# Adding a graph bias once, as a constant matrix in VectorE's copy, in place of bias matmuls in the coefficient steps

## What is computed

```python
# stage 1: eight Euler steps, linear in h
h = x @ fc_in_w.T + fc_in_b
alph = sigmoid(alpha_train)[:, None]
w_eff = w * clip(d, 0, 1) @ w.T
for _ in range(8):
    ax = adj @ h                                   # over nodes
    f = alph * 0.5 * (ax - h) + h @ w_eff - h + x0 # x0 = x
    h = h + 0.125 * f
x = layernorm(x + h)
# stage 2: four-head attention, 32 channels a head, edges with adj == 0 masked
q, k, v = split(x @ W)
out = softmax(q @ k.T / sqrt(32) + mask) @ v
x = layernorm(x + out)
```

## Time and profile before

| what | value |
|---|---|
| median of three runs | 682.69 us |
| the profiled execution | 683.51 us |
| its span, first to last instruction | 681.7 us |
| instructions in the span | 11846 |
| TensorE matmuls | 646.5 us busy, 95%, 3441 matmuls |
| VectorE, ScalarE, GpSimd | 456.5, 452.1 and 72.9 us busy |
| distance of the items' first PV, 180 to 625 us | 37.1 us, twelve times (one 37.3) |
| chain that ended last | TensorE 85%, VectorE 8%, issue 3% |
| mean granted TensorE clock | 0.989 of full |

### The profile page before, as it was taken

The page is one execution under the profiler, slowest core; times in us unless marked ns, Lnnn a source line. Parts: engine busy times, 40 slices in busy tenths (PEclk is TensorE's granted clock), DMA queues, the critical chain, the costliest instruction groups (busy, mean ns, idle before and its releaser), DMA issues.

```text
span 681.7 us, 11846 instructions
## 1 busy us (share of the span) xinstructions
PE 646.5 (95%) x3441; PEld 474.3 (70%) x3441; DVE 456.5 (67%) x1308; ACT 452.1 (66%) x1023; POOL 72.9 (11%) x86
## 2 busy tenths in 40 slices
PE   4998799999999999999999999999999999999883
PEld 3776676867777776868686777778686868676541
DVE  3442437568594958677685849485866768496986
ACT  3122146867778686868686776868686868678881
POOL 3110000001010100101010102001010101000001
PEclk9999999999999999999999999999999999999897
DMA  4000021312213130403031221303030312112211
GB/s 112 0 1 16 0 63 47 78 33 67 59 43 83 25 101 12 112 0 100 24 82 41 63 60 36 88 19 104 11 103 10 96 27 73 37 49 62 65 29 48
DMA packets 37695, 35.47 MB, mean 52 GB/s; under 512 B 7840, under 2 KB 24864, under 8 KB 37664
## 3 DMA queue, kind: packets, MB, share of 16 engines
q1 hardware_dynamic: 37664, 35.09, 20.0%
HBM read 5.57 MB, written 4.19 MB: 14 GB/s over the span
## 4 chain that ended last, share of the span: by engine, by line
PE 85%; DVE 8%; issue 3%; ACT 1%; DMA 1%; SPq 0%; POOL 0%; DVEq 0%; POOLq 0%
PE psS L711 9%; PE psO L816 8%; PE psL L697 8%; PE psL L698 8%; PE psL L699 8%; PE psE L801 7%; PE psL L689 5%; PE psL L691 5%; PE psL L690 5%; PE psM L771 4%; PE psE L797 4%; PE psL L762 2%; PE psM L776 2%; PE psS L636 2%; PE psE L636 2%
## 5 line engine op out<-in xcount | busy, mean ns | idle before, releaser
L957 DVE CUSTOM_DVE_ANT_0 Sm<-psS,mask 128x512 f32<-128x512 f32 x256 | 173.1, 687 | 109.2 <-PE psS L711 66.4
L545 ACT ACTIVATE E<-Sm,negmax 128x512 f32<-128x512 f32 x128 | 91.5, 715 | 39.7 <-DVE negmax L957 39.5
L711 PE MATMUL psS<-Ks,Qs 96*128 96x512 f32 x256 | 99.7, 447 | 4.5 <-DVE negmax L957 2.4
L545 ACT ACTIVATE Sm<-Sm,negmax 128x512 f32<-128x512 f32 x128 | 92.4, 727 | 6.6 <-DVE negmax L957 6.6
L588 ACT ACTIVATE ET<-ET 128x512 f32<-128x512 f32 x128 | 77.7, 622 | 0.4 <-DVE ET L992 0.3
L992 DVE TENSOR_TENSOR ET<-psE,maskT 128x512 f32<-128x512 f32 x120 | 77.0, 682 | 1.0 <-PE psE L797 1.0
L478 POOL TENSOR_TENSOR rstd<-var,minus_half 128x4 f32<-128x4 f32 x32 | 32.2, 1007 | 364.9 <-DVE var L940 364.9
L801 PE MATMUL psE<-ident,E 128*128 128x128 f32 x480 | 67.8, 275 | 2.3 <-ACT ET L591 1.5
L591 ACT ACTIVATE ET<-psE 128x512 f32<-128x512 f32 x116 | 68.5, 590 | 0.3 <-PE psE L801 0.3
L711 PEld LDWEIGHTS psS<-Ks,Qs 96*128 96x128 f32 x256 | 45.6, 192 | 28.7 <-issue 14.2
L801 PEld LDWEIGHTS psE<-ident,E 128*128 128x128 f32 x480 | 57.3, 142 | 8.5 <-ACT E L545 1.7
(11 more groups left out here) (158 smaller groups left out, 1100.7 us busy)
## 6 DMA issues: line engine op xcount, KB each, us to landing
Qs<-qh SPq DMA_DIRECT2D x128, 64.0 KB, 2.0
Ks<-kh SPq DMA_DIRECT2D x128, 64.0 KB, 2.0
xin<-in_x_dram SPq DMA_DIRECT2D x16, 256.0 KB, 2.9
...
Qs<-Mh SPq DMA_DIRECT2D x16, 4.0 KB
```

What stands on the lines that cost most here:

```text
L545: nc.scalar.activation(row if h < TH else E[:, h % 2, i, :], row, ACT.Exp, scale=-1.0, bias=negmax[:, h * NT + i:h * NT + i + 1], accum_ou ...
L711: mm(psS[i % 2][:, :], Qs[0:KS, h, i * P:(i + 1) * P], Ks[0:KS, h, :], start=True, stop=True).then_inc(s_mm, 1)
L957: V_.tensor_tensor_reduce(out=Sm[:, i % 2, :], in0=psS[i % 2][:, :], in1=mask[:, i, :], scale=-SCALE, scalar=3e38, op0=ALU.add, op1=ALU.mi ...
```

## The change

The whole bias becomes one 128 by 512 constant `biasT`. It is worked out in the preamble and in pass 0, by matmuls that lie between the units of item 0, and VectorE adds it as it copies `J1` to `YT`. `J0` stays with ScalarE. The matmul of line 684 is gone from all coefficient steps, and so are the factors `rb` and `Wst`. All lists are written anew.

TensorE:

```diff
-            for i in range(PW):
-                for k in range(NT if i else 1):
-                    for part in (PTh, PTl) if i else (spread,):
-                        last = mm(psM[0:3 * QUAD, :], sel[:, i, 0:3 * QUAD], ...
+            def bias_columns(q, pick):
+                rows = slice(q * QUAD, q * QUAD + pick.shape[0])
+                pe.wait_ge(bias_ev, (3, 7)[q])
+                n = pick.shape[1]
+                for t in range(NT):
+                    last = mm(psM[:, t * n:(t + 1) * n], wrow[rows, t * P:(t + 1) * P], pick,
+                              start=True, stop=True)
+                last.then_inc(bias_mm, 1)
+            def bias_rows(q):
+                pe.wait_ge(bias_ev, (2, 6, 9)[q])
+                for k in range(NT):
+                    for part in (PTh, PTl):
+                        last = mm(psM[0:3 * QUAD, :], wcols[q][:, k, 0:3 * QUAD], part[:, PW - 1 if q else 0, k, :],
+                                  start=k == 0 and part is PTh, stop=k == NT - 1 and part is PTl)
+                last.then_inc(bias_mm, 1)
+            def bias_constant():
+                pe.wait_ge(bias_ev, 10)
+                mm(psM[:, :], brow[:, :], wrow[:, :], start=True, stop=True).then_inc(bias_mm, 1)
...
             recurrence(7)
+            bias_rows(0)
             power(2, 1)
...
             power(2, 2)
-            for q in range(BLK):
-                last = mm(psM[0:3 * QUAD, q * D:(q + 1) * D], bcols[:, q, :], ident[:, :], start=True, stop=True)
+            bias_columns(0, fold[0:PW, 0:PW - 1])
+            mm(psM[0:3 * QUAD + 1, P:P + D], bcols[:, :], ident[:, :], start=True, stop=True).then_inc(bias_mm, 1)
...
             def coefficients(it, block):
-                mm(bank, rb[0:3 * QUAD, block, :], Wst[0:3 * QUAD, :], start=True, stop=False)
                 for i in range(PW):
-                    mm(bank, Rh[:, k, :], zh[:, i, :], start=False, stop=False)
+                    mm(bank, Rh[:, k, :], zh[:, i, :], start=i == 0, stop=False)
...
+                        # apply_power calls this between its 6th and 7th matmul, in J1 of item 0
+                        bias_constant if first and n else None
...
+                        if (kind, n) == ("YT", 0):
+                            bias_rows(1)
+                        elif (kind, n) == ("J", 0):
+                            bias_columns(1, fold[QUAD:QUAD + 2 * PW, :])
+                        elif (kind, n) == ("YT", 1):
+                            bias_rows(2)
```

VectorE (pass 0, and the join of every item). In the preamble it also gets two small operations on `wcols`, six small copies and three small operations in place of three copies, and `bias_row`, `bias_split` and a copy to `brow` in place of two subtractions:

```diff
+                        if (kind, n) == ("YT", 1):
+                            bias_row(4, slice(QUAD, QUAD + 2 * PW))
+                            bias_split(2, 5)
+                        elif (kind, n) == ("J", 1):
+                            bias_row(6, slice(2 * QUAD, 2 * QUAD + 2 * PW))
+                            dve.wait_ge(bias_mm, 7)
+                            V_.tensor_copy(biasT[:, :], psM[:, :]).then_inc(bias_ev, 1)
+                            dve.wait_ge(bias_ev, 11)
...
+                    elif kind == "J":
+                        dve.wait_ge(l0_mm, l0_unit(b, (kind, n)) + 1)
+                        bank = L0_BANK[L0_UNITS.index((kind, n))]
+                        V_.tensor_tensor(YT[:, :], psL[bank][:, :], biasT[:, :], ALU.add).then_inc(l0_ev[bank], 1)
```

The lists, new order from the start of a pass (the drain lists are written anew too):

```diff
+PE_EVENTS = [
+    ("S", 2, 0, 2), ("S", 2, 1, 2), ("PV", 0, 0, 3), ("PV", 1, 0, 3), ("PV", 2, 0, 3), ("MT", 0, 0, 2),
+    ("PV", 3, 0, 3), ("S", 2, 2, 2), ("UT", 0, 0, 1), ("Z", 1, 0, 0), ("TR", 0, 0, 2), ("TR", 0, 1, 2),
+    ("XT", 0, 0, 0), ("S", 2, 3, 2), ("X1T", 0, 0, 1), ("CB", 0, 0, 3), ("S", 3, 0, 2), ("TR", 0, 2, 2),
+    ("S", 3, 1, 2), ("Q", 1, 0, 1), ("Z", 2, 0, 0), ("TR", 0, 3, 2), ("S", 3, 2, 2), ("K", 2, 0, 1),
+    ("TR", 1, 0, 2), ("TR", 1, 1, 2), ("C", 2, 0, 0), ("S", 3, 3, 2), ("TR", 1, 2, 2), ("TR", 1, 3, 2),
...
+ACT_EVENTS = [
+    ("TR", 3, 2, 3), ("S", 1, 3, 2), ("TR", 3, 3, 3), ("MT", 0, 0, 2), ("OT", 0, 0, 3), ("S", 2, 0, 2),
+    ("S", 2, 1, 2), ("Z", 1, 0, 0), ("X1T", 0, 0, 1), ("S", 2, 2, 2), ("S", 2, 3, 2), ("XT", 0, 0, 0),
+    ("TR", 0, 0, 2), ("TR", 0, 1, 2), ("Q", 1, 0, 1), ("TR", 0, 2, 2), ("S", 3, 0, 2), ("TR", 0, 3, 2),
...
+DVE_EVENTS = [
+    ("TR", 3, 2, 3), ("MT", 0, 0, 2), ("S", 2, 1, 2), ("LN1A", 0, 0, 1), ("TR", 3, 3, 3), ("S", 2, 2, 2),
+    ("LN1B", 0, 0, 1), ("TR", 0, 0, 2), ("S", 2, 3, 2), ("Z", 1, 0, 0), ("TR", 0, 1, 2), ("S", 3, 0, 2),
+    ("S", 3, 1, 2), ("XT", 0, 0, 0), ("TR", 0, 2, 2), ("QL", 1, 0, 1), ("TR", 0, 3, 2), ("TR", 1, 0, 2),
...
+    ("S", 1, 3, 1), ("J", 1, 0, 0), ("TR", 3, 1, 2), ("S", 2, 0, 1),
...
-    ("XS", 0, 0, 0), ("LN1A", 0, 0, 0), ("KEEP", 0, 0, 0), ("LN2A", 0, 0, 2),
+    ("XS", 0, 0, 0), ("LN1A", 0, 0, 0), ("LN2A", 0, 0, 2), ("KEEP", 0, 0, 0),
...
-    ("STK", 0, 0, 2), ("STK", 1, 0, 2), ("OUT", 0, 0, 4), ("STK", 2, 0, 2), ("STK", 3, 0, 2), ("XIN", 0, 0, 0),
-    ("MT", 0, 0, 2),
+    ("XIN", 0, 0, 0), ("STK", 1, 0, 2), ("STK", 2, 0, 2), ("OUT", 0, 0, 4), ("STK", 3, 0, 2), ("MT", 0, 0, 2),
+    ("STK", 0, 0, 1),
```

More of the change, by code:

```diff
@@ L208, in gnn_kernel @@
         Rl = sb("Rl", [P, RS, D], F32R)
-        rb = sb("rb", [P, BLK, D], F32R)
-        Wst = sb("Wst", [P, N], F32R)
+        biasT = sb("biasT", [P, N])
+        brow = sb("brow", [3 * QUAD + 1, D])
+        fold = sb("fold", [2 * QUAD, PW])
+        rowsum = sb("rowsum", [P, NT])
         W_sb = sb("W_sb", [P, 3 * D])
@@ L243, in gnn_kernel @@
         decay_ident = x1res[:, 1, 3, :]
-        bcols = bass.AP(x1res, NT * D, [list(x1res[:, 0, 0, :].ap[0]), [3 * QUAD, BLK], [1, 3 * QUAD]])
+        bcols = x1res[:, 1, 0, 0:3 * QUAD + 1]
         Sm = sb("Sm", [P, 2, N])
@@ L260, in gnn_kernel @@
         minus_half = sb("minus_half", [P, NT])
+        wrow = att[0:3 * QUAD + 1, :, :].rearrange("p t d -> p (t d)")
+        wcols = [t[:, :].rearrange("p (t c) -> p t c", c=P) for t in (kh, qh, ql)]
         Rst = bass.AP(ET, 0, [list(ET[:, 0, 0, :].ap[0]), [(RS + 1) * SLOT, 2], [SLOT, RS + 1], [1, SLOT]])
@@ L306, in gnn_kernel @@
         bias_mm = sem("bias_mm")
-        bias_hi = sem("bias_hi")
-        bias_lo = sem("bias_lo")
+        bias_ev = sem("bias_ev")
+        w_sum = sem("w_sum")
         xin_in = [sem("xin_in0"), sem("xin_in1")]
@@ L450, in _ @@
             nc.gpsimd.memset(Rst[:, :, 0, :], 0.0).then_inc(c_pool, 1)
-            nc.gpsimd.memset(bcols[:, :, :], 0.0).then_inc(c_pool, 1)
-            nc.gpsimd.memset(f(sel[:, :, :]), 0.0).then_inc(c_pool, 1)
-            nc.gpsimd.memset(f(spread[:, :]), 1.0 / P).then_inc(c_pool, 1)
+            nc.gpsimd.memset(bcols[:, :], 0.0).then_inc(c_pool, 1)
+            for t in (kh, qh, ql):
+                nc.gpsimd.memset(f(t[:, :]), 0.0).then_inc(c_pool, 1)
+            nc.gpsimd.memset(att[:, :, :], 0.0).then_inc(c_pool, 1)
             nc.gpsimd.memset(minus_half[:, :], -0.5).then_inc(c_pow, 1)
             pool.wait_ge(c_pow, 1)
-            pool.wait_ge(c_pool, 6)
-            for i in range(PW):
-                nc.gpsimd.memset(f(sel[:, i, :]).rearrange("p (h r) -> p h r", r=QUAD)[:, 0:3, i:RS:PW],
-                                 1.0).then_inc(c_pool, 1)
+            pool.wait_ge(c_pool, 8)
+            nc.gpsimd.memset(f(wcols[0][:, :, 0:1]), 1.0).then_inc(c_pool, 1)
+            nc.gpsimd.memset(f(wcols[1][:, :, QUAD:QUAD + 1]), 1.0).then_inc(c_pool, 1)
+            pool.wait_ge(c_pool, 10)
+            nc.gpsimd.memset(wrow[3 * QUAD:3 * QUAD + 1, :], 1.0).then_inc(c_pool, 1)
+            pool.wait_ge(c_pool, 11)
             pool.wait_ge(p_sb, NT)
@@ L506, in _, with row_sum @@
                 nc.scalar.activation(Ph[:, t, :], P_sb[:, t, :], ACT.Copy).then_inc(p_hi, 1)
+            def row_sum(t):
+                nc.scalar.activation(ET[:, H - 1, t, :], P_sb[:, t, :], ACT.Copy,
+                                     accum_out=rowsum[:, t:t + 1]).then_inc(w_sum, 1)
             def power_high(i, m):
@@ L514, in _ @@
                     power_high(i, m)
+                    if i == 1 and m < NT - 1:
+                        for t in range(2 * m, min(2 * m + 2, NT)):
+                            row_sum(t)
             def split_x(parity, loads):
@@ L656, in _ @@
             recurrence(7)
-            pe.wait_ge(c_pool, 9)
-            for i in range(PW):
-                for k in range(NT if i else 1):
-                    for part in (PTh, PTl) if i else (spread,):
-                        last = mm(psM[0:3 * QUAD, :], sel[:, i, 0:3 * QUAD],
-                                  part[:, i - 1, k, :] if i else repeated(part[:, :], N // D),
-                                  start=i == 0, stop=i == PW - 1 and k == NT - 1 and part is PTl)
-            last.then_inc(bias_mm, 1)
+            bias_rows(0)
             power(2, 1)
@@ L692, in coefficients, with apply_power @@
                 return last
-            def apply_power(bank, high, low, i, fresh):
+            def apply_power(bank, high, low, i, fresh, between=None):
                 for k in range(NT):
+                    if k == 2 and between:
```

(52 more changed lines are left out.)

21 lines of the change are left out of this document (5 added, 16 removed), and 113 rows, old and new, of tables (ACT_DRAIN, ACT_EVENTS, DVE_DRAIN, DVE_EVENTS).

## The result

The changed kernel is slower: 698.1 us (median of four runs, 697.8 to 699.3) against 682.9 (681.0 to 684.9) of the kernel before, a ratio of 1.0225 with a 95% interval of [1.0194, 1.0257]. The profiled execution took 697.77 us.

A forecast was written before the change was run, and what follows sets the result against it. TensorE, busy 95% of the span, was taken as the bound. Passes 2 to 15 -5.0, preamble -1.8, item 0 +1.4, pass 1 +0.6, drain 0: sum -4.8, thus 677.9 us on the median, range 672.0 to 682.5.

The forecast's parts named there:

- the rest of the list: Other reordered entries of an item: KEEP and XS on GpSimd cost nothing, three close places 0.07 us (-0.1 to +0.6).
- Bias matmuls: On TensorE, 48 bias matmuls, 3 an item, go at 0.23 us each: a gain of 0.70 us an item.
- X1T closer to UT: On TensorE, less work between UT and X1T, so X1T waits 0.60 us, not 0.33: 0.27 us an item lost.
- Other close places: QL ahead of K, YT0 ahead of J0, S10's maximum ahead of S12: tight margins, priced at 0.07 us an item.
- the three terms: Per full item: -0.70 for bias matmuls, +0.27 for X1T's wait, +0.07 for tight places; sum -0.36, thus 36.8 us.
- Rival B: No change, 682.7 us: K, J0 or S12 on TensorE waits 0.35 us more in each item; chance 0.13.
- J1's copy on VectorE: J1's copy moves from ScalarE (0.60 us) to VectorE (0.68), covered by idle time, so it costs nothing.
- Rival C: Slower, 686.3 us if MT's DMA lands at 4.0 us: TR00 waits for its second row; chance 0.07.
- Preamble and item 0: Preamble: fewer matmuls, -1.8 us (-2.1 to -1.3); item 0: new bias work minus three bias matmuls, +1.4 (0 to 2.5).
- Pass 1: VectorE's bias addition to J1 delays mask and moments, X1T 1.3 us later, three matmuls fewer: +0.6 us (0 to 1.5).
- rival D: Clock halves for 6.9 us behind pass 1's longer X1T wait, costing 3.4 us once: 681.3 us; chance 0.06.

The follow-up runs named there:

- the run with the small operations: Changed kernel, lists kept, GpSimd's KEEP copy and XS subtraction cut to one of 128 columns; 683.9 us, ratio 0.9998 to the kernel before.
- the run with the old lists: New bias arithmetic under the lists of the kernel before, only J1 moved from ScalarE's to VectorE's; 677.8 us, ratio 0.9912 to the kernel before.

## Why the prediction was wrong

The forecast was 677.9 us with a range from 672.0 to 682.5; the result is 698.1. The sign was wrong.

**The step that failed** is in the part on the rest of the list: "KEEP goes behind LN2A on GpSimd, and XS behind both, which still ends before the next Z1." All of that is true, and none of it was the question. I asked who waits for the two operations and priced them at nothing. I didn't ask what runs on VectorE in the same 1.9 us. The new lists put LN2B there, 1.1 us of operations that both read and write SBUF, and GpSimd's hold stretches them to 2.30. That cost 14.1 of the 19.1 us missed (1.17 us an item in the mean), by the run with the small operations. The trace of before didn't show this collision in a full item, but it had a hint in the preamble: a VectorE copy of 128x130 took 1.15 us (19.09 to 20.24) where two like it later take 0.22 each, beside a run of GpSimd subtractions that ended at 20.14.

**Bias matmuls.** The price was right, the gain a little smaller. In the item of the earlier trace rows and the same item of the run with the old lists (UT at 258.26 and 258.77), YT0 stands behind two of the three places and starts 17.34 us behind UT before and 16.86 without the matmuls, 0.24 for each. By the 131 ns at 512 columns of the Trainium skill, TensorE: Matmul & The Clock Gate, section Back-to-back issue gap, an estimate for the two is 0.26 us, and the runs show 0.48. At the V products 0.15 of it is given back, for a reason that I haven't found, and an item gains 0.55 in all, not 0.70.

**X1T closer to UT.** Right to a hundredth. The timeline of TensorE in the changed kernel:

```profile
265.27 0.60 PE L785 MATMUL psM<-ident,YT 128*128 128x128 f32 x4
...
270.24 0.63 PE L790 MATMUL psM<-ident,x 128*128 128x128 f32 x4 [0.42 <-DVE x L999]
```

UT to X1T is 4.97 us (forecast 4.96), and the idle part 0.42 was forecast at 0.4 to 0.5.

**Other close places.** Without the collision the items take 36.77 or 36.82 us against 36.8, and the one wait of TensorE that recurs there is the one ahead of X1T. So the sum of the three terms held, in part by luck: the first gave 0.55 and not 0.70, and no run takes the 0.07 put on QL, YT0 and the maximum of S10 by itself. Rival B was right that TensorE would wait for VectorE. It named K, J0 and S12 as the places, and the waits stand ahead of S10 and S11, a pair of tiles before S12. It priced a slip of 0.35 from tight order, and the held LN2B made it 1.2, far beyond the range.

**J1's copy on VectorE.** Right: 692 ns, with 20.4 us of idle time ahead of the sixteen (the group above), and no wait of TensorE behind it.

**Rival C**, the DMA of MT: refuted. TensorE waits for no DMA ahead of TR00.

**Preamble and item 0.** Forecast -1.8 and +1.4. (The terms of the first, -2.1 and +0.4, give -1.7.) Measured by the first Z1 (53.05 to 52.04) -1.0, and from there to UT +1.9. The sum is 1.3 us off. Part of it is the same collision. The timelines of GpSimd and VectorE of the changed kernel:

```profile
34.28 1.30 POOL L474 TENSOR_TENSOR Xl<-xin,Xh 128x512 fp32r<-128x512 f32 x1 [14.20 <-ACT Xh L530]
35.63 1.80 POOL L478 MEMSET Ks<- 2x2048 f32 x1
...
35.77 1.75 DVE L903 COPY ET<-ET 128x130 f32<-128x130 f32 x1
35.90 1.63 DVE L931 CAST kh<-rowsum 128x4 fp32r<-128x4 f32 x1
37.58 0.17 DVE L933 TENSOR_TENSOR kh<-rowsum,kh 128x4 fp32r<-128x4 f32 x1
```

Beside GpSimd's clearing of `Ks`, which ran at 43.20 in the kernel before, a copy takes 1.75 us in place of 0.22 and a cast of four columns 1.63. TensorE waits 0.21 us for that copy, and bias_rows(0) behind it starts 0.43 us later than the bias matmuls did in the kernel before. I had called these small operations free in idle time. The rest is not worth a cause: between executions whose preamble is the same, UT of item 0 moves by about as much (78.95 in the kernel before and 79.69 in the same kernel with LN2B moved; 79.87 to 80.91 with the new arithmetic and the new lists).

**Pass 1 and rival D.** Forecast +0.6, measured +3.6. X1T starts 7.11 us behind UT (5.76 before), the +1.3 that was forecast. Three matmuls fewer were to give back 0.7. The rest is rival D, which came true beside the main loss: 6.83 us at 0.50 of the clock start at 87.41, between these two rows of TensorE's timeline:

```profile
86.98 0.69 PE L790 MATMUL psM<-ident,x 128*128 128x128 f32 x4 [3.26 <-DVE x L999]
88.36 2.08 PE L794 MATMUL psM<-x1T,W_sb 128*128 128x512 f32 x2 [0.69 <-ACT x1T L574]
```

It was priced at 3.4 us and cost up to 2.9 (3.6 less 1.35, plus the 0.7 that the matmuls were to give back). I held it as a rival to the forecast with 0.06, where it was an addition to whatever else happened.

**What stays open.** With the collision gone and the new lists kept, the ratio is 0.997 or 0.9998, where the forecast was 0.993. What is missing lies ahead of pass 2. The old lists were better for this arithmetic than the new ones by 0.3 us an item. That fits the wait ahead of X1T, 0.42 us an item in the new lists without the collision and 0.12 in the old ones (0.27 more was forecast). But the runs that took this wait away gained 0.1 us at most, as another came in its place, so what the old lists do better stays open.
